# Experts' tiles and the scan's chunks in one order, with the rows fetched through a table that TensorE makes

## The reference, cut to what matters

```python
x = layernorm(L0_x)                       # xn: (1024, 256)
# the scan's branch
h = rmsnorm(x) * norm_scale
z, xs, B, C, dt = split(h @ in_proj_w)    # 512, 512, 128, 128, 4 heads
xs = silu(conv4(xs) + conv_bias);  dt = softplus(dt + dt_bias)
log_a = -exp(A_log) * dt
y = ssd_scan(log_a, B, C, dt, xs) + D * xs     # chunked: inside a chunk by masked decays,
                                               # between chunks by a carried state
s = x + (y * silu(z)) @ out_proj_w
# the experts' branch
top2 = top_k(x @ gate_w.T, 2);  w = softmax(top2 values)
e_out = sum over the token's 2 experts of w * (silu(x @ fc1[e].T) * (x @ fc2[e].T)) @ proj[e].T
x1 = L0_x + s * silu(e_out)
# layer 1 (not changed): layernorm, attention of 32 heads over 8 KV heads, a second mixing, residuals
```

## Time and profile before

| | us |
|---|---|
| median of 3 runs | 830.13 (828.55 to 831.89) |
| the profiled execution's own time | 831.76 |
| its span | 829.9 |
| scan, from the first transfer of rows to the last product | 72.5 to 149.3 |
| first hidden layer of a tile starts | 160.92 |
| last projection of a tile ends | 348.39 |
| DVE goes on behind the second barrier | 367.65 |
| PE busy, share of the span | 720.9, 87% |

### The profile page before, as it was taken

The page is one execution under the profiler, slowest core; times in us unless marked ns, Lnnn a source line. Parts: engine busy times, 40 slices in busy tenths (PEclk is TensorE's granted clock), DMA queues, the critical chain, the costliest instruction groups (busy, mean ns, idle before and its releaser), DMA issues.

```text
span 829.9 us, 13253 instructions
## 1 busy us (share of the span) xinstructions
PE 720.9 (87%) x4503; PEld 626.7 (76%) x4504; DVE 495.9 (60%) x1003; ACT 401.5 (48%) x1029; POOL 409.6 (49%) x459
## 2 busy tenths in 40 slices
PE   1997587479999999808868999999999999999995
PEld 1884465479999999706657888888888888888874
DVE  7786587112322222177746677777777777777764
ACT  3644231211221211224545767666776766676663
POOL 3334886101111011112567777777777777777550
PEclk9989799689999999958989999999999999999999
DMA  9100000699999998142622422233222223222001
GB/s 306 30 1 19 32 27 26 203 289 353 344 336 295 294 308 249 56 135 60 193 77 52 118 62 71 64 77 83 70 65 68 64 68 84 70 66 63 8 1 51
DMA packets 112867, 100.33 MB, mean 121 GB/s; under 512 B 56960, under 2 KB 83264, under 8 KB 112672
## 3 DMA queue, kind: packets, MB, share of 16 engines
q1 hardware_dynamic: 110416, 94.36, 39.3%
q0 software_dynamic: 2384, 5.13, 1.7%
HBM read 69.27 MB, written 13.41 MB: 100 GB/s over the span
## 4 chain that ended last, share of the span: by engine, by line
PE 57%; DVE 14%; POOL 10%; ACT 7%; issue 5%; DMA 3%; SPq 2%; POOLq 0%; DVEq 0%; ACTq 0%
PE bank L1519 12%; PE bank L1539 7%; PE bank L1377 7%; PE bank L1379 7%; PE bank L1378 7%; PE bank L1373 6%; POOL prob L1335 5%; ACT prob L1157 3%; PE bank L1619 3%; DVE nmax L915 2%; PE bank L1620 2%; POOL q_lo L1347 2%; DMA to_row<-slot_row 2%; ACT kv_hi L1164 1%; DVE o_lo L928 1%
## 5 line engine op out<-in xcount | busy, mean ns | idle before, releaser
L1335 POOL TENSOR_TENSOR prob<-prob,rinv 128x128 f32<-128x128 f32 (+3 forms) x256 | 177.8, 725 | 104.2 <-DVE rinv L920 104.2
L1157 ACT ACTIVATE prob<-bank,nmax 128x512 f32<-128x512 f32 (+3 forms) x256 | 133.4, 529 | 45.6 <-DVE nmax L915 44.2
L924 DVE TENSOR_TENSOR kv_lo<-bank,kv_hi 128x512 fp32r<-128x512 f32 x160 | 110.2, 689 | 52.7 <-ACT kv_hi L1164 51.8
L1164 ACT ACTIVATE kv_hi<-bank 128x512 fp32r<-128x512 f32 x160 | 96.4, 602 | 80.6 <-PE bank L1373 80.6
L1519 PE MATMUL bank<-xgT,wm 128*128 128x128 f32 x920 | 108.8, 279 | 0.0
L1519 PEld LDWEIGHTS bank<-xgT,wm 128*128 128x128 f32 x920 | 107.1, 196 | 0.1
L1304 POOL DMA_INDIRECT y_rows<-y_row,to_row x23 | 22.4, 976 | 171.0 <-DVE y_row L806 171.0
L1373 PE MATMUL bank<-cst,prob 128*128 128x128 f32 x640 | 97.4, 275 | 3.0 <-ACT prob L1157 1.2
L915 DVE TENSOR_REDUCE nmax<-bank 128x1 f32<-128x512 f32 (+2 forms) x192 | 91.4, 504 | 13.6 <-PE bank L1622 12.9
L1619 PE MATMUL bank<-kT,qT 128*128 128x512 f32 (+3 forms) x256 | 82.3, 327 | 13.2 <-ACT prob L1157 7.1
L1377 PE MATMUL bank<-kv_hi,v_lo 128*128 128x128 f32 (+3 forms) x256 | 92.8, 362 | 0.3 <-DVE kv_lo L924 0.3
(11 more groups left out here) (283 smaller groups left out, 1513.6 us busy)
## 6 DMA issues: line engine op xcount, KB each, us to landing
wm<-in_w_moe SPq DMA_DIRECT2D x23, 1280.0 KB, 6.2
wm<-in_w_moe SPq DMA_DIRECT2D x23, 640.0 KB, 6.0
qT<-q_hi SPq DMA_DIRECT2D x124, 64.0 KB, 2.0
qT<-q_lo SPq DMA_DIRECT2D x124, 64.0 KB, 2.0
k_exp<-k_rows SPq DMA_DIRECT2D x56, 64.0 KB, 2.0
x_sorted<-zeros SPq DMA_DIRECT2D x1, 2944.0 KB, 11.9
wtl<-in_w_moe_tail SPq DMA_DIRECT2D x46, 64.0 KB, 5.6
xg<-x_sorted SPq DMA_DIRECT2D x1, 2432.0 KB, 14.8
```

The costliest lines, as they stand in the source:

```text
L924: TT(p_lo[:, b_, :], bank[2 + b_ % 2][:, :], p_hi[:, b_, :].bitcast(F32), ALU.subtract).then_inc(plo_done, 1)
L1157: ins = actv(prob[:, i % 2, h, POFF[j]:POFF[j] + (j + 1) * P], bk[:, at:at + (j + 1) * P], ACT.Exp, bias=nmax[:, i % 2, h, j:j + 1], accum ...
L1335: ins = GT(seg, seg, rinv[:, i % 2, k, j:j + 1].to_broadcast([P, (j + 1) * P]), ALU.mult)
```

## The change

Scan and tiles stand in one order. `side_by_side` lists every step with a position (a tile has four units of the axis, `4 * j`), sorts the list, and all four computing engines take their own steps from it. `CHUNK_AT` puts chunk 0 ahead of the tiles, the other seven 13 units (3.25 tiles) apart, the last reaching into tile 22. The barrier between scan and tiles is gone. Tiles use banks 0 to 3 and chunks banks 4 to 7, so that every buffer of a chunk and every bank of a tile is single: `hidden` of tile j+1 needs each of its banks read by ACT or DVE in tile j, and bank 3 holds both the projection and the turned rows. PE's order within a tile is hidden part 1, turn of j+1, parts 2 and 3, projection of j-1.

The rows are not sent. SP writes `xn_tok` to `xn_rows` once, early. DVE (`ask_table`) makes for each pair a one-hot of its lane and, three times, a one-hot of its tile multiplied by the target row, the token's number and the weight; 16 matmuls of 69 columns (`make_table`) sum these into a table by lane and tile, which `take_table` reads back as `from_row`, `to_row` and `tab`. POOL then fetches each tile's 128 rows by one indirect transfer, three tiles ahead (`fetch`, `XR` = 4 buffers). Weights are asked for as soon as `owner` is known. K's and V's weights are loaded after the rows' return, and split at the end of layer 0, ahead of the barrier that remains. SBUF is laid out by hand (`Map`), because scan and tiles must now fit beside each other.

```diff
+def side_by_side():
+    z = []
+    for j in range(NJ + 1):
+        at = 4 * j
+        if j < NJ:
+            z += [(at, "PE", "H1", j), (at + 0.1, "ACT", "H1", j), (at + 1, "PE", "H2", j), (at + 1.1, "DVE", "H2", j),
+                  (at + 2, "PE", "H3", j), (at + 2.1, "ACT", "H3", j), (at + 2.2, "DVE", "H3", j)]
+        if j + 1 < NJ:
+            z += [(at + 0.9, "PE", "X", j + 1), (at + 1, "ACT", "X", j + 1)]
+        if j + XR - 1 < NJ:
+            z += [(at + 0.2, "POOL", "X", j + XR - 1)]
+        if j > 0:
+            z += [(at + 3.1, "PE", "P", j - 1), (at + 3.2, "DVE", "P", j - 1), (at + 3.3, "POOL", "P", j - 1)]
...
+    for c in range(NT):
+        a = CHUNK_AT[c]
+        z += [(a - 4, "POOL", "D", c), (a + 0.5, "PE", "F", c), (a + 1, "ACT", "F", c), (a + 1.5, "PE", "C", c), (a + 2, "ACT", "C", c),
+              (a + 2.5, "DVE", "C", c), (a + 3, "POOL", "C", c), (a + 5.5, "PE", "Y", c), (a + 6.5, "DVE", "Y", c), (a + 7.4, "ACT", "O", c),
+              (a + 8.4, "DVE", "L", c)]
...
+CHUNK_AT = [-10] + [4 + 13 * c for c in range(NT - 1)]
...
-            sp.wait_ge(pool_ready, 1)
-            sp.dma_start(x_sorted.rearrange("(j p) c -> p j c", p=P),
-                         zeros[:, :].unsqueeze(1).to_broadcast([P, NJ, C])).then_inc(scratch_in, 16)
...
-            end_phase(sp)
+            sp.wait_ge(xn_ready, NT)
+            sp.dma_start(xn_rows.rearrange("(t p) c -> p t c", p=P), xn_tok[:, :, :]).then_inc(xn_out, 16)
...
+            sp.wait_ge(w_lo_done, 2)
+            sp.wait_ge(owner_ready, 1)
+            for j in range(3):
+                expert_rows(j)
...
+            def ask_table():
+                rows = [P, NT * 2, NJ]
+                dve.wait_ge(pr_full, BATCH * len(PROJS))
+                then(TT(reached[:, :, :], slot_f[:, :].unsqueeze(2).to_broadcast([P, NT * 2, NJ + 1]),
+                        edges.unsqueeze(1).to_broadcast([P, NT * 2, NJ + 1]), ALU.is_ge))
+                then(vec.reduce_sum(in_lane[:, :].unsqueeze(2), reached[:, :, :], axis=AX.X))
...
+                TT(lanes[:, :, :], in_lane[:, :].unsqueeze(2).to_broadcast([P, NT * 2, P]),
+                   lane_no.unsqueeze(1).to_broadcast([P, NT * 2, P]), ALU.is_equal).then_inc(table_ready, 1)
+                then(TT(in_tile[:, :, :], reached[:, :, 0:NJ], reached[:, :, 1:NJ + 1], ALU.subtract))
...
+                for i, what in enumerate((row_no, token_no, weight_f[:, :, :].rearrange("p t k -> p (t k)"))):
+                    TT(sel[:, :, i, :], in_tile[:, :, :], what.unsqueeze(2).to_broadcast(rows), ALU.mult).then_inc(table_ready, 1)
...
+            def make_table():
+                pe.wait_ge(table_ready, 4)
+                for r in range(NT * 2):
+                    ins = mm(bank[0][:, 0:3 * NJ], lanes[:, r, :], sel[:, r, :, :].rearrange("p i j -> p (i j)"), start=r == 0, stop=r == NT * 2 - 1)
...
+            def fetch(j):
+                if j == 0:
+                    gp_.wait_ge(rows_ready, 2)
+                    gp_.wait_ge(xn_out, 16)
+                if j >= XR:
+                    gp_.wait_ge(xg_full, j - XR + 1)
+                pool.indirect_dma_start(out=xg[:, j % XR, :], out_offset=None, in_=xn_rows,
+                                        in_offset=bass.IndirectOffsetOnAxis(ap=from_row[:, j:j + 1], axis=0)).then_inc(xg_in[j % XR], 16)
...
             def turn_x(j):
+                pe.wait_ge(xg_in[j % XR], 16 * (j // XR + 1))
+                if j > 2:
+                    pe.wait_ge(row_taken, j - 2)
...
             def project(j):
+                pe.wait_ge(xgT_ready, min(j + 3, NJ))
...
+            act.wait_ge(kv_in, 96)
+            actv(kv_raw[:, 0, :, 0:2 * P], kv_raw[:, 0, :, 0:2 * P], ACT.Copy, scale=HD ** -0.5).then_inc(k_scaled, 1)
+            actv(kv_hi[:, 1, :, :], kv_raw[:, 1, :, :], ACT.Copy)
             end_phase(act)
```

More of the change, by code:

```diff
@@ L50 @@
 NJ = 2 * T // P + E - 1
+XR = 4
 SLOTS = NJ * P
@@ new lines, in layered_kernel @@
+        owner_f = first("owner_f", [P, NJ])
+        spare_f = first("spare_f", [P, NJ])
+        assert first.at <= weights_at
+        w_out_sb = Map(weights_at)("w_out_sb", [P, NCH, C])
+        table = Map(hT_at)
+        reached = table("reached", [P, NT * 2, NJ + 1])
+        in_tile = table("in_tile", [P, NT * 2, NJ])
+        lanes = table("lanes", [P, NT * 2, P])
+        sel = table("sel", [P, NT * 2, 3, NJ])
+        assert table.at <= hT_at + 2 * KC * T * 4 + NCH * (TAPS - 1 + SEQ) * 4
@@ new lines, in counted @@
+        def counted(t):
+            ends = [0, NJ + 1, NJ + 1 + P, NJ + 1 + P + 2 * NT, NJ + 1 + P + 4 * NT, 2 * NJ + 1 + P + 4 * NT]
+            return [t[:, i:j] for i, j in zip(ends, ends[1:])]
+        edges, lane_no, row_no, token_no, spare_no = counted(count_f)
+        scan = Map(both.at)
+        decay_in = scan("decay_in", [P, NH, P])
+        w_end = scan("w_end", [P, NH])
+        dx = scan("dx", [P, NCH, P])
+        state = scan("state", [P, NH, P])
+        within = scan("within", [P, NH, P])
@@ new lines, in layered_kernel @@
+        since = scan("since", [P, NH, P])
+        cbm = scan("cbm", [P, P])
+        mix = scan("mix", [P, NH, P])
+        c_dec = scan("c_dec", [P, NH, P])
+        x_dt = scan("x_dt", [P, NH, P])
+        x_end = scan("x_end", [P, NH, P])
+        y_hi = scan("y_hi", [P, NCH, P], F32R)
+        y_lo = scan("y_lo", [P, NCH, P], F32R)
+        wsg = scan("wsg", [P, KC, C])
+        wcen = scan("wcen", [P, KC, C])
+        wst = scan("wst", [P, KC, 4])
+        rp = scan("rp", [P, TB, 2, HD])
@@ new lines, in layered_kernel @@
+        rp4 = turns[:, :, :].rearrange("p i (t h d) -> p i t h d", t=TB, h=4)
+        assert scan.at <= hT_at
+        tiles = Map(hT_at)
+        xg = tiles("xg", [P, XR, C])
+        xgT = tiles("xgT", [P, 2, KC, P])
+        sil = tiles("sil", [P, 2, HC * P])
+        hE = tiles("hE", [P, 2, HC * P])
+        y_row = tiles("y_row", [P, 2, C])
+        assert tiles.at <= weights_at
+        weights = Map(weights_at)
+        wm = weights("wm", [P, 3, FULL, WM])
+        wtl = weights("wtl", [P, 3, KC, P])
@@ L737, in _ @@
                         dve.wait_ge(conv_done, (TAPS - 1) * n + j + 1)
[L738 removed]
             place_tokens()
[L741 to L749 removed]
+            ask_table()
```

702 lines of the change are left out of this document (340 added, 362 removed).

## The result

The changed kernel takes **805.07** us (median of 4 runs, 803.47 to 805.53) against 830.23 before (4 runs). The ratio is 0.9705, 95% interval [0.9672, 0.9737]. The forecast was 808. The profiled execution took 803.47 us, its span is 801.7 us, its mean clock 0.958.

What follows compares the result with a forecast made beforehand. Tiles were taken as bound by TensorE, the scan by its engine-to-engine chain. Last projection at 90.6 + 226.8 + 5 = 322.4, 26.0 earlier, less 3.6 on the way out: 809.4 from 831.76, in medians 808; range 797 to 826.

Steps and rivals of the forecast that it cites:

- counting on PE ends: Ahead of the tiles: projections and counting on TensorE end at 66.3 us, with nothing before that getting longer.
- table on PE: Ahead of the tiles: the table's 16 matmuls, 32 passes on TensorE, take 5.1 us, 8.6 at half the clock.
- take_table, gather, turn, copy: From table to first hidden layer: small operations 1.5 us, POOL's gather 5.9, PE's turn 0.66, ACT's copy about 0.4.
- tiles and chunks, work: TensorE's work: 23 tiles at 7.72 us, a cold first tile, seven chunks at 6.45, chunk 0's output product; 226.8 us.
- stalls inside: Among the tiles: TensorE waits for y_row at bank 3, mostly at chunks 1 and 5; 5 us, bounds 1 and 20.
- behind the barrier: From DVE's start behind the second barrier to the span's end: as long as before, 462 us.
- rival of blocking: Among the tiles: DVE and POOL block each other and this reaches PE; 842 us, slower, chance 0.08.
- longer price of a table load: At chunks 1 and 5: ACT's table switch costs 2.66 us, not 1.28, so 1.4 more each; 811 in all.
- The way out: Last projection to barrier: K and V loads and splits come late, POOL ending last; 3.6 us given back, bounds 0.5 and 9.
- the chain stays exposed: Chunks beside tiles: each keeps its 3.2 us of idleness because banks and buffers are single; 825 us, chance 0.20.
- more is hidden: Start, stage and way out: gather lands in 2.4 us, no stalls, way out at 0.5; 796 us, chance 0.08.
- three signs of being wrong: Tiles' pace away from chunks above 8 us, start past 97, or what follows the barrier not as long as before.

Runs made afterwards that it cites:

- scan_behind: The changed kernel with chunks 1 to 7 placed behind the last tile in the same order list; 880.1 us, ratio 1.0638.
- warm: The changed kernel with 32 and 26 unused identity matmuls filling TensorE's idleness ahead of the table and of tile 0's turn; 804.43 us, ratio 0.968.
- way_out_no_drain: The changed kernel with POOL's drain ahead of the barrier replaced by a wait for its last subtraction's signal and a plain increment; 802.46 us, ratio 0.9675.

## Why the prediction was right

| step | forecast | measured | difference |
|---|---|---|---|
| counting on PE ends | 66.3 | 62.2 | -4.1 |
| counts to owner | 4.0 | 3.8 | -0.2 |
| ask_table | 6.7 | 6.4 | -0.3 |
| table on PE | 5.1 (4.3 to 8.6) | 7.1 | +2.0 |
| take_table, gather, turn, copy | 8.5 | 9.1 | +0.6 |
| first hidden layer | 90.6 | 88.7 | -1.9 |
| tiles and chunks, work | 226.8 | 226.4 | -0.4 |
| stalls inside | 5 (1 to 20) | 1.0 | -4.0 |
| last projection to barrier | 22.9 | 26.6 | +3.7 |
| behind the barrier | 462.2 | 459.0 | -3.2 |
| the execution's own time | 809.4 | 803.5 | -5.9 |

*The mechanism* held. Tiles go on at 7.72 us and a chunk beside them costs its own matmuls: the work came out at 226.4 for a forecast of 226.8. `scan_behind` shows that the chain of a chunk, 17.5 us by itself, is hidden but for these matmuls and the stalls below.

*Stalls* were placed rightly and sized too large: "I take 5 us, bounds 1 and 20". Only chunks 1 and 5 wait, 0.51 each, where I worked out 0.85 from the order and up to 2.2 more from POOL beside `w_end`. That second term came to nothing: `w_end` was over at 107.68 and POOL's mix started at 107.75, and `x_dt` and `x_end`, which lie beside mix and c_dec and read a bank, took 0.69 and 0.68. The rival of blocking falls with it: the gate's product has a median of 692 ns. The longer price of a table load, 811 in all, did not come either: such a load takes 1.28 us again and the next instruction starts directly behind it (330.74 + 1.28, next at 332.04).

*The table* was mis-sized: I took 5.1 from a group at the full clock and one cold comparison. PE had stood still 7.8 us and the whole table was cold, 7.1. `warm` shows 3.8 at the full clock, so either end of my bounds was a state of the clock, and the idleness ahead of it, which I had named, decided which.

*The way out* is the step that failed most. "Only then can the barrier open" left out that POOL's last subtraction is followed by its own drain. Before, POOL had long been idle at the barrier, so the drain was hidden; now it stands last, for 3.9 us (`way_out_no_drain`). The 3.6 us themselves were right in sum (POOL's end at 338.81 is 22.75 behind the last projection, forecast 22.9), though of the loads in it the four small ones took SP 3.74 us for my 2 and the two large ones 1.62 for my 3.15.

*What I had not seen at all* is the clock. My start of 66.3 and the 462 us behind the barrier came from one profile in which the clock fell early. This made the forecast for the profiled execution 4.1 too late; the other 3.2 behind the barrier go the same way in part. The clock falls for some microseconds at changing times there, and the rest spreads from 457.8 to 460.5 over the ten profiles of kernels built on the changed one in which this part was left alone. But the two built on the kernel before have 462.2 and 462.9. So some 2 us remain that I can't put down to anything. "Not as long as before" was one of my three signs of being wrong, and by 3.2 us it came about.

The rival "the chain stays exposed" (825) is refuted by the 1.0 us of idleness, "more is hidden" (796) had the stalls right and the gather and the way out wrong. The forecast of 808 missed by 2.9, and closer than the sum was. Its errors, -4.1, -4.0, -3.2 and +3.7, +2.0, partly cancel. And the 5.9 of the profiled execution shrank to 2.9 only because that execution was 1.6 below its median, where the one that I started from was 1.6 above. So the mechanism was right, and the closeness of the number is in part luck.

## What to carry to other kernels

A stage that is bound by hand-overs and one that is bound by TensorE can be laid side by side at the price of the first one's matmuls, and single buffers did little harm then, 1.0 us of waiting here; the same chunks by themselves, in the same order, took 17.5 us each. Work moved to the last place ahead of a barrier costs its own length and the drain of its engine, so ask which engine arrives last and with what in flight, and whether what you move behind the barrier blocks a neighbour there. Read a clock from more than one profile before building a sum on the time at which something ends.
